# Graph layer over 64 items: where the second squares and the inverse norms are turned along the rows, and where group 0's residual is formed

## The reference, cut to what matters

```python
def reference(x, adj, bias, W_lang, W_grav, W_V, W_O, gate_logit, log_sigma):
    h = _layernorm(x + L0(x, adj, bias), axis=-1)   # L0: a graph over the 512 nodes, 153 nearest kept, adj as the weight
    z_l, z_g, v = h @ W_lang.T, h @ W_grav.T, h @ W_V.T              # per item, 128 x 512 each
    zn  = z_l / jnp.maximum(norm(z_l), EPS)
    A_l = jnp.maximum(zn @ zn.T, 0.0) * not_eye
    sq  = jnp.sum(z_g * z_g, axis=-1, keepdims=True)
    d2  = jnp.maximum(sq + sq.T - 2.0 * (z_g @ z_g.T), 0.0)
    A_g = jnp.exp(-d2 / (2.0 * sigma * sigma)) * not_eye
    K   = w_l * row_stochastic_causal(A_l) + (1.0 - w_l) * row_stochastic_causal(A_g)
    return _layernorm(h + (K @ v) @ W_O.T, axis=-1)
```

## Time and profile before

| | |
|---|---|
| runs, median (3) | 951.38 us |
| the profiled execution's own time | 956.53 us |
| its span, first to last instruction | 954.8 us |
| TensorE busy | 921.0 us, 96% |
| VectorE busy | 752.5 us, 79% |
| ScalarE busy | 535.4 us, 56% |
| GpSimd busy | 312.8 us, 33% |
| DMA queue, share of 16 engines | 27.4% |
| mean granted TensorE clock | 0.989 of full |

### The profile page before, as it was taken

How to read it: one execution, slowest core, us unless ns; L and a number is a source line. 1 busy time by engine, 2 the same in 40 slices (tenths; PEclk the granted TensorE clock), 3 DMA queues, 4 the chain that set the end, 5 groups by cost and what they waited for, 6 DMA issues and landing times.

```text
span 954.8 us, 19036 instructions
## 1 busy us (share of the span) xinstructions
PE 921.0 (96%) x6858; PEld 542.5 (57%) x6858; DVE 752.5 (79%) x1716; ACT 535.4 (56%) x976; POOL 312.8 (33%) x435
## 2 busy tenths in 40 slices
PE   8999899899999999999999999999999999999993
PEld 7777787455555555556464646455555455555451
DVE  5887488768888888878787888888887878786766
ACT  6887556685555555555546464646373636463531
POOL 5888162244040404040505050505050504040410
PEclk9999899999999999999999999999999999999997
DMA  7554120001323232314141413232222323231211
GB/s 301 187 204 150 43 90 25 34 32 21 80 67 78 67 83 60 95 48 109 34 120 28 115 33 109 40 103 46 96 53 90 57 86 60 85 56 45 56 45 44
DMA packets 101848, 75.84 MB, mean 79 GB/s; under 512 B 80560, under 2 KB 80688, under 8 KB 99888
## 3 DMA queue, kind: packets, MB, share of 16 engines
q1 hardware_dynamic: 101808, 75.32, 27.4%
HBM read 38.86 MB, written 16.78 MB: 58 GB/s over the span
## 4 chain that ended last, share of the span: by engine, by line
issue 51%; PE 21%; POOL 14%; DVE 8%; ACT 5%; DMA 1%; POOLq 1%; DVEq 0%; ACTq 0%
POOL arena L438 6%; PE bank L265 2%; PE bank L267 2%; PE bank L266 2%; PE bank L538 2%; POOL arena L443 2%; POOL arena L477 2%; PE bank L545 1%; PE bank L544 1%; ACT arena L1188 1%; POOL rn_parts L460 1%; DVE stats L1692 1%; POOL part_rest L458 1%; PE bank L508 1%; PE pair L265 1%
## 5 line engine op out<-in xcount | busy, mean ns | idle before, releaser
L265 PE MATMUL bank<-arena 128*128 128x512 f16 (+2 forms) x1056 | 293.8, 302 | 7.3 <-DVE arena L1746 2.7
L267 PE MATMUL bank<-arena 128*128 128x512 f16 (+2 forms) x1056 | 293.5, 302 | 0.0
L266 PE MATMUL bank<-arena 128*128 128x512 f16 (+2 forms) x1056 | 293.5, 302 | 0.0
L265 PE MATMUL pair<-arena 128*128 128x512 f16 (+1 forms) x400 | 151.1, 378 | 0.0
L266 PE MATMUL pair<-arena 128*128 128x512 f16 (+1 forms) x400 | 150.8, 377 | 0.0
L267 PE MATMUL pair<-arena 128*128 128x512 f16 (+1 forms) x400 | 150.7, 377 | 0.0
L265 PEld LDWEIGHTS bank<-arena 128*128 128x128 f16 x1056 | 103.5, 98 | 69.4 <-DVE arena L1746 5.0
L267 PEld LDWEIGHTS bank<-arena 128*128 128x128 f16 x1056 | 103.7, 98 | 63.3 <-issue 0.3
L266 PEld LDWEIGHTS bank<-arena 128*128 128x128 f16 x1056 | 103.7, 98 | 54.7 <-issue 0.3
L460 POOL TENSOR_TENSOR sq_parts<-cf,zero 128x4 bf16<-128x4 f32 x16 | 3.3, 208 | 399.4 <-DVE cf L1795 399.4
L438 POOL TENSOR_TENSOR arena<-arena 128x512 f32<-128x512 f32 x64 | 81.0, 1267 | 60.2 <-ACT arena L1098 59.8
(11 more groups left out here) (344 smaller groups left out, 1943.0 us busy)
## 6 DMA issues: line engine op xcount, KB each, us to landing
arena<-in_x SPq DMA_DIRECT2D x32, 1024.0 KB, 5.5
out_dram<-arena SPq DMA_DIRECT2D x15, 1024.0 KB, 4.3
arena<-arena SPq DMA_TRANSPOSE x75, 3.2
arena<-in_x SPq DMA_DIRECT2D x2, 512.0 KB, 4.6
arena<-in_w_grav_t SPq DMA_DIRECT2D x1, 1024.0 KB, 7.3
arena<-in_w_lang_t SPq DMA_DIRECT2D x1, 1024.0 KB, 5.2
arena<-in_w_v SPq DMA_DIRECT2D x1, 1024.0 KB, 8.2
arena<-in_w_o_t SPq DMA_DIRECT2D x1, 1024.0 KB, 9.1
```

The costliest lines, as they stand in the source:

```text
L265: pe.matmul(dst, ah, bh, start=start, stop=False)
L266: pe.matmul(dst, ah, bl, start=False, stop=False)
L267: return pe.matmul(dst, al, bh, start=False, stop=stop)
```

## The change

Five things are done.

1. **Squares.** VectorE takes the diagonal of half of T_g straight out of bank 5 when `half_products` is done, and forms `dev` = half minus the row's own diagonal (one new 128x512 instruction). ScalarE and VectorE split `dev` instead of the half, so that `add_turned` adds it transposed: the bank gets the gram less the column's half-square. The four `along_rows` matmuls, the `part_rows` matmul, the split on GpSimd and ScalarE's copy go. `HALF_DOWN` and the constant `HK` are scaled to match.
2. **Inverse norms.** SP writes `nl[:, 5, :]` (128x4) to a DRAM tensor `rn_dram` and reads it back as one row for every partition (`rn_row`, 128x512, in the order residuals lie in: rows first, items inside). VectorE waits for `rn_in` in place of `rm_ps`. Again five matmuls, a split and a copy go.
3. **Mask.** T_l is masked where it lies, in bank 4, instead of into an SBUF tile, and later than before.
4. **Orders.** On TensorE `mix_nodes(g+1, 0)` goes ahead of both `add_turned`. On VectorE one of the two `x_low` ahead of `z_low(0, ...)` and the other three later ones are spread out; `first_stats`, `v_low(0)` and `first_factors(g+1, 1)` move behind other steps. On ScalarE the logarithm and exponential of the norms go ahead of `add_bias(g+1, 0)`, and K's high part ahead of two of the norms of h.
5. **Group 0's y.** ScalarE adds the bias to x in SBUF early (`x_biased`, two instructions of 128x1024); VectorE then makes y in one instruction out of PSUM (`first_y`). ScalarE's four `add_bias` and GpSimd's four residuals of group 0 go, and `upper_out(0, ...)` and `hT_high` are put in another order.

```diff
 # SyncE
+            def inverses_along(g):
+                sp.wait_ge(s["r_ready"], g + 1)
+                sp.dma_start(rn_dram, nl[:, 5, :]).then_inc(s["rn_out"], 16)
+                sp.wait_ge(s["rn_out"], g * 16 + 16)
+                sp.dma_start(rn_row.rearrange("p b n -> p (b n)"),
+                             rn_dram.rearrange("(o n) b -> o (n b)", o=1).broadcast_to([P, N4])).then_inc(s["rn_in"], 16)
             load_x(2, 0)
+            inverses_along(0)
             turn_h(1, 1)
...
                 store(g - 1)
+                inverses_along(g)
                 if g + 1 < NG:
                     turn_h(g + 1, (g + 1) % 2)
 # GpSimd
-            pool.memset(zero[:], 0.0).then_inc(cs, 1)
-            pool.memset(pick_item[:], 1.0).then_inc(cs, 1)
...
-                pool.wait_ge(s["dg_ready"], g * 2 + 2)
-                part(g, cf[:, 1, :], sq_parts, s["sq_rows_ps"], (s["part_steps"], 0), s["sq_parted"])
                 if has_next:
-                    residual(g + 1, 1 - slot, 0)
-                pool.wait_ge(s["r_ready"], g + 1)
-                pool.wait_ge(s["sq_parted"], g + 1)
-                part(g, nl[:, 5, :], rn_parts, s["rn_rows_ps"], (s["part_steps"], 4), s["rn_parted"])
-                if has_next:
-                    residual(g + 1, 1 - slot, 1)
-                    residual(g + 1, 1 - slot, 2)
+                    for b in range(GB - 1):
+                        residual(g + 1, 1 - slot, b)
 # TensorE
+                between(0)
                 pe.wait_ge(s["half_g_l_ready"], g + 1)
                 add_turned(1, s["gg_ps"])
-                between(0)
                 pe.wait_ge(s["half_l_l_ready"], g + 1)
                 add_turned(0, s["gl_ps"])
-                between(1, range(0, 1))
-
-                pe.wait_ge(s["sq_parted"], g + 1)
-                part_rows(0, sq_parts, s["sq_rows_ps"])
-                between(1, range(1, 3))
-                squares_along(g)
-                between(1, range(3, KB))
+                between(1)
                 between(2)
-
-                pe.wait_ge(s["rn_parted"], g + 1)
-                part_rows(P, rn_parts, s["rn_rows_ps"])
-                between(3, range(0, 2))
-                inverses_along(g)
-                between(3, range(2, KB))
+                between(3)
 # ScalarE
+            def x_biased(items):
+                act.activation(xg[0][:, items, :], xg[0][:, items, :], ACT.Identity,
+                               bias=bias_c[:]).then_inc(s["x_biased"], 1)
...
-                half_high(1, s["half_g_ps"], s["half_g_h_ready"])
-                half_high(0, s["half_l_ps"], s["half_l_h_ready"])
+                half_high(1, dev, s["dev_ready"], s["half_g_h_ready"])
+                half_high(0, bank[4][:].rearrange("p (b n) -> p b n", b=GB), s["half_l_ps"], s["half_l_h_ready"])
+                log_exp(g, nl, s["nl_in"], s["nl_log"], s["nl_exp"])
                 if has_next:
                     add_bias(g + 1, 0)
-                act.wait_ge(s["sq_rows_ps"], g + 1)
-                wait(act, s["sq_ps"], g)
-                act.activation(sq_rows[:], bank[6][0:GB * PARTS, 0:P], ACT.Copy,
-                               scale=-0.5).then_inc(s["sq_rows_ready"], 1)
-                log_exp(g, nl, s["nl_in"], s["nl_log"], s["nl_exp"])
 # VectorE, in the loop
-                    x_low(g + 2, slot, range(0, HALF))
+                    x_low(g + 2, slot, range(0, 1))
...
+                dve.wait_ge(s["half_g_ps"], g + 1)
                 dve.tensor_tensor(diag_g, gg, for_items(ident[:]), ALU.mult).then_inc(s["dg_ready"], 1)
...
+                dve.tensor_tensor(dev, gg, per_item(cf[:, 1, :]), ALU.subtract).then_inc(s["dev_ready"], 1)
...
-                dve.scalar_tensor_tensor(t_l, gl, 0.0, for_items(mask[:]), ALU.max, ALU.mult).then_inc(gs, 1)
...
+                dve.wait_ge(s["gl_ps"], g + 1)
+                dve.scalar_tensor_tensor(gl, gl, 0.0, for_items(mask[:]), ALU.max, ALU.mult).then_inc(gs, 1)
...
-                dve.wait_ge(s["rm_ps"], g + 1)
-                dve.tensor_tensor(a_l, t_l, bank[7][:].rearrange("p (b n) -> p b n", b=GB), ALU.mult).then_inc(gs, 1)
+                dve.wait_ge(s["rn_in"], g * 16 + 16)
+                dve.tensor_tensor(a_l, gl, rn_row.rearrange("p b n -> p (b n)").rearrange("p (n b) -> p b n", b=GB),
+                                  ALU.mult).then_inc(gs, 1)
 # VectorE, before the loop
+            def first_y(b):
+                dve.wait_ge(s["mix_ps"], b + 1)
+                dve.scalar_tensor_tensor(y[:, b, :], bank[b][:], c1(ALPHA_C), xg[0][:, b, :], ALU.mult,
+                                         ALU.add).then_inc(s["y_ready"], 1)
```

More of the change, by code:

```diff
@@ L98, in build @@
         ones = sb("ones", [P, P])
-        ident_b = sb("ident_b", [P, P], BF16)
         ident_up = sb("ident_up", [P, P], F16)
[L101 to L108, removed]
+        rn_dram = nc.dram_tensor("rn_dram", [P, GB], F32, kind="Internal").ap()
         item_of = sb("item_of", [P, CB])
@@ L235, in build @@
         tile_at = iter(range(88 * KIB, 110 * KIB, 2 * KIB))
-        diag_l, diag_g, t_l, a_l, e_g, a_g, k_g, k_mix = (
-            at(next(tile_at), [GB, P]) for _ in range(8))
+        diag_l, diag_g, dev, a_l, e_g, a_g, k_g, k_mix, rn_row = (
+            at(next(tile_at), [GB, P]) for _ in range(9))
         k_parts = at(100 * KIB, [2 * GB, P], F16)
@@ L443, in low_h @@
                 pool.tensor_tensor(h_l[:, b, :], h[slot][:, b, :], h_h[:, b, :], ALU.subtract).then_inc(s["hl_ready"], 1)
-            for b in range(GB):
-                residual(0, 0, b)
             upper_low(1, 0)
@@ L765, in values @@
                     mm.then_inc(s["v_ps"], 1)
-            def part_rows(first, parts, done):
-                pe.matmul(bank[6][0:GB * PARTS, first:first + P], parts[:].rearrange("p b i -> p (b i)"), ident_b[:],
-                          start=True, stop=True).then_inc(done, 1)
-            def along_rows(dst, rows, start, done):
-                for b in range(GB):
-                    mm = pe.matmul(dst[:, b * P:(b + 1) * P], pick_item[:, b, :], rows[:], start=(start and b == 0),
-                                   stop=(b == GB - 1), skip_group_check=True)
-                mm.then_inc(done, 1)
             def weighted(g, b):
@@ L1297, in _ @@
             act.activation(vo_scale[:, 0:1], vo_scale[:, 1:2], ACT.Exp, scale=0.5).then_inc(s["vo_root"], 1)
-            first_roots(0, 1)
-            upper_out(0, 0)
-            first_norm(0, 0, 2)
-            first_norm(0, 0, 3)
-            for b in range(GB):
-                hT_high(b)
-            for d in range(1, KB):
+            for d in range(KB):
                 upper_out(0, d)
@@ L1796, in body @@
                 dve.wait_ge(s["dg_ready"], g * 2 + 2)
+                dve.tensor_tensor(dev, gg, per_item(cf[:, 1, :]), ALU.subtract).then_inc(s["dev_ready"], 1)
                 dve.tensor_scalar(cf[:, 0, :], cf[:, 1, :], c1(HK), None, ALU.mult).then_inc(s["hk_ready"], 1)
-                dve.wait_ge(s["gl_ps"], g + 1)
+                if has_second:
+                    x_low(g + 2, slot, range(1 if has_previous else 0, 2))
+                dve.wait_ge(s["half_g_h_ready"], g + 1)
+                half_low(1, dev, s["half_g_l_ready"])
+                dve.wait_ge(s["half_l_h_ready"], g + 1)
                 dve.tensor_tensor(diag_l, gl, for_items(ident[:]), ALU.mult).then_inc(s["nl_steps"], 1)
+                half_low(0, gl, s["half_l_l_ready"])
                 dve.wait_ge(s["nl_steps"], g * 2 + 1)
@@ L1850, in body @@
                 if has_next:
-                    first_factors(g + 1, 1)
-                v_low(0)
+                    first_stats(g + 1, 3)
+                    first_moments(g + 1, 1)
                 dve.wait_ge(s["cl_ready"], g + 1)
@@ L1859, in body @@
                 last.then_inc(s["k_ready"], 1)
+                if has_next:
+                    first_factors(g + 1, 1)
+                v_low(0)
                 if has_next:
```

160 lines of the change are left out of this document (71 added, 89 removed).

## The result

The changed kernel takes 971.36 us (median of 4 runs, 970.37 to 972.56) beside 951.31 for the kernel before on the same chip: ratio 1.0203, 95% interval 1.0183 to 1.0222. It is **slower by 2.0%**, where 921.6 us, faster by 3.1%, was forecast, with a range up to 934. Its profiled execution took 972.04 us itself, so it stands for the median well.

A forecast was written before the change was run, and what follows sets the result against it. TensorE, busy 921.0 of 954.8 us, was taken as the bound. Savings of 20.3 + 2.4 + 1.8 + 3.5 + 0.5 + 1.3 = 29.8 us took the median from 951.38 to 921.6 us, own range 918 to 929, wider range 916 to 934.

The forecast's parts named there:

- Small matmuls, 20.3 us: TensorE, 15 groups: removing ten small matmuls and the holes around them saves 1.35 us a group, 20.3 us.
- (b): Rival, TensorE: only the small matmuls' columns are saved, holes stay; 0.56 us a group, 933.5 us in all; chance 7%.
- (d): Rival, TensorE's instruction orders: the change does not remove the ten matmuls a group; excluded, no chance given.
- VectorE in time for `add_turned`: VectorE's `half_low` parts come before TensorE wants them, margins 1.4 and 0.6 us: no wait, no cost.
- Rival (c): VectorE late for `add_turned` by contention or `x_low` in its way: 1.0 us a group, 937.6 us; chance 8%.
- Round trip 5.6 us: Inverse norms written and read back by two DMAs, 2 x (2.4 + 0.4) us, landing about 1 us before A_l.
- Rival (a): The inverse norms' DMA round trip becomes the wait: free up to 9 us, 967 us total at 12; chance 3%.
- K at 612.3, 2.0 us of slack: VectorE ends K at 612.3 instead of 615.5; its transpose lands about 2.0 us before TensorE wants it.
- `x_low`, 2.4 us: One `x_low` less ahead of the last `z_low` that TensorE waits for: 12 x 0.2 = 2.4 us saved.
- the DMA waits, 1.8: TensorE's two DMA-transpose waits: K's in group 14 shrinks from 1.8 to about 0.6 us, h's goes; 1.8 us saved.
- Group 0, 3.5 us: Ahead of group 0, y by `first_y` shortens TensorE's wait and avoids a slower clock: 3.5 us of 3.1 to 4.4.
- Last group, 1.3 us: Last group, where TensorE waits for K: K 2.0 us earlier, but one more `v_low` before its low part; 1.3 us.

The follow-up runs named there:

- d4: Changed kernel, every group's y by VectorE from PSUM, `v_high(1)` earlier, `xw_low` behind two second residuals, next factors then `x_low(3)` behind K: 938.10 us, 0.9831 of the kernel before.
- a4: Changed kernel with the inverse norms stored by item, 512 values of 4 bytes instead of 128 of 16: 1031.14 us, ratio 1.0814 to the kernel before.
- a1: Changed kernel with GpSimd's residual of groups 1 to 15 over 4 of 512 columns, leaving out most of x: 938.31 us, ratio 0.9836 to the kernel before.
- d2: Changed kernel, every group's y by VectorE from PSUM, `v_high(1)` earlier, `xw_low` behind two second residuals, `x_low(3)` then next factors behind K: 946.23 us, 0.9915 of the kernel before.
- b1: Kernel before with only group 0's y by VectorE, ScalarE's bias on x and their order: 949.93 us beside 953.07, ratio 0.9966.
- c1: Kernel before with only the inverse norms sent by DMA through memory, squares as before: 960.24 us, ratio 1.0073 to the kernel before.

## Why the prediction was wrong

- **Small matmuls, 20.3 us: right, and not enough.** They and their holes are gone (busy time 19.3 us less; d4's period is 45.9 us with 0.6 of gaps in it). Rivals (b) and (d) are out. The rule that (b) names holds in a stream of 128-column matmuls, whose starts are 0.056 us apart in the kernel before (592.81 to 592.87); what it leaves out are the holes around small matmuls among wide ones.
- **VectorE in time for `add_turned`: right.** `half_low` of T_g and T_l end 3.7 and 4.9 us after the last `z_low`; 4.0 and 5.2 were worked out. Rival (c) had the wrong place, but one of its two causes, contention, was the one that counted, further down the chain.
- **Round trip 5.6 us: right**, 5.35 from issue to landing (1.4 + 3.9, not 2 x 2.4). The prediction's other price, 2.0 us fixed for each, is not borne out by the small store, which lands in 1.4. Rival (a) is out for 15 groups; a4 shows its price.
- **K at 612.3, 2.0 us of slack: the step that failed.** The sum took VectorE's instructions at the lengths that they had in the old places. That GpSimd's residuals only come forward was taken for free; they come forward by up to 1.4 us, the head of VectorE's chain (the cap) by 2.4, and the two now lie beside each other. Stretched instructions cost 5.45 us there (1.8 before); a1, with the residuals short, has K 2.2 us earlier. A_l's step cost 0.4, and its slack was spent. K's measured place is +23.5 for +19.6.
- **What nothing in the sum asked:** how much slack y2 had. It was 0.45 us, less than the 1.35 taken from TensorE, and this wait was in no rival. K just in time for TensorE is not enough: a1 has K at +21.3 and no wait for it, waits for y2 and is at 938, not 921.6. By theory V (an estimate, from 45.3, 15.8 and the 9.03 us behind K) K had to end by about +20.5, so at +19.6 it had 0.9 us of slack and not 2.0. At +19.6 y2 would not have been waited for by this; no run has K that early (d2 to d4 have +22.1, with `xw_low` moved out of the path). By theory V the removal alone, with VectorE's path as it was, was worth an estimated 46.93 - (30.56 + 15.81) = 0.56 us a group, 8 us instead of 20.
- **`x_low`, 2.4 us, and the DMA waits, 1.8:** the waits for `z_low` went as forecast, but time won there is lost again at y2; of the DMA waits the one in group 14 has grown from 1.8 to 3.2 us, where 0.6 was forecast.
- **Group 0, 3.5 us: right** (b1, 3.1). **Last group, 1.3 us:** TensorE waited 2.48 us for K instead of 2.62, so 0.1. There the cause is the round trip: no residual lies beside the chain, and VectorE waits 2.97 us for the row.

The split between the two parts of a group is not complete: the norms alone cost 7 us (c1); the squares alone were not tried.

## What to carry to other kernels

When work is taken off the engine that bounds, don't stop at its waits: measure the margin of every hand-over to it, also where no wait is listed, since the smallest one caps the gain. And when an order moves, check VectorE's instructions against GpSimd's row by row: those with two SBUF inputs, and small `tensor_scalar` ones, belong where GpSimd rests, those out of PSUM, sums and `bn_stats` may lie beside its work. An addition that GpSimd does "for free" can cost more than VectorE doing it out of PSUM.

## What was not expected of the hardware

- An instruction of VectorE on 2 columns takes 0.15 us or 1.22, by whether GpSimd is in an addition of 128x512; making 60 such additions short gave this kernel 33 us back (a1).
- A store of 2 KB takes 1.4 us in 128 pieces of 16 bytes and 9.0 in 512 of 4 (a4); reading at a step of 16 bytes makes a 128x512 product 1.08 us for 0.69.
- From the issue of K's transpose to TensorE's first use are 3.1 us (changed kernel); a pair of h's transposes takes 4.7 us from issue until `project_z` starts (d2).
